# Inverses of the 32-row blocks made on VectorE, column by column, between the links of a running substitution

## What is computed

```python
s = jnp.einsum('bihd,bjhd->bhij', k, k) * scale
s = jnp.where(strict, s, -jnp.inf)          # strict: i > j
...
p = e / jnp.where(denom == 0, 1.0, denom)   # softmax over the strict lower triangle
L = p * beta.transpose(0, 2, 1)[..., None]
A = L + jnp.eye(T, dtype=L.dtype)[None, None]
u = jax.scipy.linalg.solve_triangular(A, v.transpose(0, 2, 1, 3), lower=True)
...
o = jnp.einsum('bhij,bjhd->bihd', attn, u).reshape(B, T, HID)
```

## Time and profile before

| | us |
|---|---|
| median of 3 runs | 886.89 |
| lowest and highest | 881.65, 887.53 |
| the profiled execution | 889.51 |
| its span | 887.7 |
| mean granted TensorE clock in it, share of full speed | 0.731 |

### The profile page before, as it was taken

The page is one execution under the profiler, slowest core; times in us unless marked ns, Lnnn a source line. Parts: engine busy times, 40 slices in busy tenths (PEclk is TensorE's granted clock), DMA queues, the critical chain, the costliest instruction groups (busy, mean ns, idle before and its releaser), DMA issues. The chain is left out here.

```text
span 887.7 us, 17573 instructions
## 1 busy us (share of the span) xinstructions
PE 531.0 (60%) x7316; PEld 409.8 (46%) x7316; DVE 570.7 (64%) x1036; ACT 279.6 (31%) x682; POOL 230.8 (26%) x322
## 2 busy tenths in 40 slices
PE   0343752445646499633655745765988672599981
PEld 0232532334434144432544434544665451599981
DVE  6679589659795958577671776256565238378743
ACT  3330242123144344005344052242412232245520
POOL 2000000000000000030582880860681007123444
PEclk9765875775665599865658757776868855699985
DMA  8442050041000100075005004120000052646314
GB/s 317 137 93 51 1 107 0 2 85 23 1 0 13 37 1 0 16 147 126 4 27 120 7 7 98 20 44 7 9 8 11 9 236 71 251 158 220 119 53 126
DMA packets 52064, 61.27 MB, mean 69 GB/s; under 512 B 25408, under 2 KB 45392, under 8 KB 47504
## 3 DMA queue, kind: packets, MB, share of 16 engines
q1 hardware_dynamic: 50176, 55.15, 23.0%
q0 software_dynamic: 1808, 4.99, 1.9%
HBM read 45.24 MB, written 13.63 MB: 66 GB/s over the span
## 5 line engine op out<-in xcount | busy, mean ns | idle before, releaser
L778 PE MATMUL psum<-arena 32*32 32x16 f32 (+20 forms) x5480 | 368.6, 280 | 251.1 <-DVE arena L1417 67.8
L778 PEld LDWEIGHTS psum<-arena 98*32 98x32 bf16 (+7 forms) x5480 | 265.4, 128 | 354.1 <-issue 104.2
L1851 POOL TENSOR_TENSOR arena<-arena 128x31 f32<-128x31 f32 (+15 forms) x124 | 67.5, 544 | 9.7
L1849 POOL TENSOR_TENSOR arena<-arena 128x31 f32<-128x31 f32 (+15 forms) x124 | 64.2, 518 | 9.7
L1206 ACT ACTIVATE arena<-psum 128x512 f32<-128x512 f32 (+1 forms) x48 | 35.4, 737 | 62.8 <-PE psum L778 62.5
L1402 DVE RECIPROCAL arena<-arena 128x512 f32<-128x512 f32 x16 | 53.6, 3353 | 0.5
L1237 ACT ACTIVATE psum<-psum,arena 128x256 f32<-128x256 f32 (+7 forms) x128 | 45.7, 371 | 26.2 <-DVE arena L1478 26.2
L1488 DVE TENSOR_REDUCE arena<-psum 128x2 f32<-128x512 f32 (+1 forms) x48 | 41.4, 862 | 18.6 <-PE psum L778 18.3
L1149 ACT ACTIVATE arena<-arena 128x255 f32<-128x255 f32 x64 | 27.1, 495 | 72.7 <-DVE arena L1380 72.7
L1394 DVE TENSOR_TENSOR_SCAN arena<-arena 128x255 f32<-128x255 f32 x64 | 42.6, 728 | 3.6 <-ACT arena L1149 3.4
L1862 POOL TENSOR_TENSOR fc_second_parts<-arena,fc_first_parts 128x2048 fp32r<-128x2048 f32 x6 | 27.9, 4651 | 64.1 <-ACT fc_first_parts L1305 64.1
(11 more groups left out here) (176 smaller groups left out, 917.9 us busy)
## 6 DMA issues: line engine op xcount, KB each, us to landing
arena<-fc SPq DMA_DIRECT2D x16, 1024.0 KB, 5.7
arena<-parts SPq DMA_DIRECT2D x40, 256.0 KB, 4.5
parts<-arena SPq DMA_DIRECT2D x16, 384.0 KB, 3.2
arena<-parts SPq DMA_DIRECT2D x40, 128.0 KB, 5.4
dispatched<-arena SPq DMA_DIRECT2D x1, 2048.0 KB, 18.4
arena<-arena SPq DMA_DIRECT2D x128, 8.0 KB, 1.8
arena<-dispatched SPq DMA_DIRECT2D x8, 256.0 KB, 3.2
expert_rows<-arena SPq DMA_DIRECT2D x8, 256.0 KB, 2.2
```

What stands on the lines that cost most here:

```text
L778: return nc.tensor.matmul(out, lhsT, rhs, start=start, stop=stop)
L1849: link(G_.tensor_tensor(tmp, A3[:, k + 1:BLK, k:k + 1].to_broadcast([P, rows, w]), X3[:, k:k + 1, 0:w].to_broadcast([P, rows, w]), ALU.mult))
L1851: ins = G_.tensor_tensor(X3[:, k + 1:BLK, 0:w], X3[:, k + 1:BLK, 0:w], tmp, ALU.add)
```

## The change

GpSimd's part of step `blocks` is taken out. VectorE's `blocks` now also clears blkX, sets its diagonal, and multiplies blkA by cT. The 31 columns of each batch become steps `("column", b, k)`, done by VectorE: those of batch 0 in a row, right ahead of its `inverse`; those of batches 1, 2 and 3 spread by `spread` over the chain of the batch before. `lag()` is the same as before and holds a column back as it does any other step that is not in its list. The semaphore `inverses_ready` is gone.

```diff
+        if b == 0:
+            o += [("column", 0, k) for k in range(BLK - 1)]
...
-        o += sum(spread(solve, ahead[b]), [])
+        columns = one_each(("column", b + 1, k) for k in range(BLK - 1)) if b + 1 < B else []
+        o += sum(spread(spread(solve, ahead[b]), columns), [])
...
                 elif kind == "blocks":
 
                     b = step[1]
-                    if b:
-                        dve.wait_ge(inv_ready, b)
                     wait_done(dve, ("kdiag", b), "act")
-                    st(V.transpose(cT, ncc[b]))
-                    st(V.transpose(blkA.rearrange("p (i j) -> p i j", i=BLK), diag.rearrange("p (n i) -> p i n", i=BLK)))
-                    settle()
-                    V.nop().then_inc(blocks_ready, 1)
+                    st(V.memset(blkX, 0.0))
+                    link(V.transpose(cT, ncc[b]))
+                    V.transpose(blkA.rearrange("p (i j) -> p i j", i=BLK), diag.rearrange("p (n i) -> p i n", i=BLK)
+                                ).then_inc(blocks_ready, 1)
+                    dve.wait_ge(blocks_ready, b + 1)
+                    st(V.memset(blkX[:, 0:BLK * BLK:BLK + 1], 1.0))
+                    link(V.tensor_tensor(A3, A3, cT.unsqueeze(2).to_broadcast([P, BLK, BLK]), ALU.mult))
+                elif kind == "column":
+
+                    k = step[2]
+                    rows, w = BLK - 1 - k, k + 1
+                    tmp = blkT[:, 0:rows * w].rearrange("p (i j) -> p i j", i=rows)
+                    link(V.tensor_tensor(tmp, A3[:, k + 1:BLK, k:k + 1].to_broadcast([P, rows, w]),
+                                         X3[:, k:k + 1, 0:w].to_broadcast([P, rows, w]), ALU.mult))
+                    link(V.tensor_tensor(X3[:, k + 1:BLK, 0:w], X3[:, k + 1:BLK, 0:w], tmp, ALU.add))
                 elif kind == "inverse":
 
                     b = step[1]
-                    dve.wait_ge(inv_ready, b + 1)
...
-                    if b and s == 0:
-                        dve.wait_ge(u_moved, 16 * HQ * NS * b)
+                    if s == 0:
+                        dve.wait_ge(*((u_moved, 16 * HQ * NS * b) if b else (pad_ready, 1)))
...
-                elif kind == "blocks":
-
-                    b = step[1]
-                    pool.wait_ge(blocks_ready, b + 1)
-                    if b:
-                        pool.wait_ge(invT_ready, b)
```

More of the change, by code:

```diff
@@ L416, in program @@
         top[0] = max(top[0], e_end)
+        A3, X3 = (f.rearrange("p (i j) -> p i j", i=BLK) for f in (blkA, blkX))
         def oraw(layer, b):
@@ L583, in program @@
         blocks_ready = sem("blocks_ready")
-        inv_ready = sem("inverses_ready")
         invT_ready = sem("inverses_T_ready")
```

## The result

The changed kernel takes 932.8 us (median of 4 runs, 929.17 to 934.34); the kernel before took 886.07 beside it (881.65 to 887.53). The ratio is 1.053, with a 95% interval of 1.048 to 1.058: 46.7 us slower. The forecast was 57 us (944, range 921 to 970). Direction and range held; the loss was oversized by about 10 us. In time alone 932.8 lies halfway between the forecast and the first rival (922), so the time does not choose between them; the profiles have to.

The account below looks back on a forecast made before the run. VectorE was taken as already the busiest compute engine beside TensorE. 23.3 + 2.4 + (13.2 - 4.1) + (11.3 - 2.5) + (13.8 - 1.9) - 1.0 + 2.5 = 57.0 us takes the median from 886.9 to 944 us, range 921 to 970.

Parts of the forecast that it names:

- first rival: In the chains, VectorE never idles while it has columns, delays using up later waits; +35, 922 us; chance 0.18.
- the 1.0 of credit: Before 485 us, ahead of `vproj`: VectorE instructions run faster without GpSimd beside them, about 1.0 us back.
- columns ahead of chain 1's `minus`: Two columns delay the `minus` that releases TensorE's transpose L905: +1.1 us.
- columns ahead of chain 2's `minus`: Four columns ahead of this `minus` add about 2.0 us.
- Batch 0: Its 31 columns between `vproj` and `inverse` are queued behind a 17.75 us wait and have no cover: +23.3 us.
- Price of a column: Two dependent VectorE instructions, 2 x 193 ns + 2 x 1.043 n ns: 0.45 to 0.92 us, 23.3 us a batch.
- second rival: Column elements cost 1.75 ns each in this layout, +7.7 us a batch: +29, 973 us; chance 0.16.
- Step `blocks`: VectorE's added clears and product take 2.4 us, uncovered only for batch 1, ahead of its first-link copies: +2.4 us.
- The walk over the waits: Columns checked wait by wait over 13 stretches per chain: 13.2, 10.2 and 11.8 us uncovered in chains 0, 1, 2.
- What is given back: VectorE's instructions speed up without GpSimd beside them: credits 4.1, 2.5, 1.9 us in chains 0 to 2, about 1.0 earlier.
- Clock: TensorE's busy share falls in the longer chains, so its granted clock may drop: guessed 0 to 8 us, taken +2.5.
- What was to be seen: Profile signs: VectorE busy 85 us more, first `inverse` 22 us later, TensorE idle over 25, chains about 62, 62, 44 us.

Follow-up runs that it names:

- no_columns: Changed kernel with all 124 columns left out on VectorE, clears and product with cT kept, so no engine inverts: 877.44 us, ratio 0.9934 to the kernel before.
- only0: Changed kernel with only batch 0 inverted on VectorE, batches 1 to 3 on GpSimd as before: 906.95 us, ratio 1.0248 to the kernel before.
- late: Changed kernel with batches 1 to 3 inverted on VectorE, batch 0 on GpSimd: 913.55 us, ratio 1.0335 to the kernel before.
- early0: Changed kernel with batch 0's columns moved forward, 6 behind batch 1's key maxima, 25 in front of batch 2's `vproj`: 908.65 us, ratio 1.0314 to before.
- placed: Changed kernel with columns of batches 1 to 3 hand-placed ahead of updates, the rest ahead of the inverse: 922.9 us, ratio 1.0472 to the kernel before.
- gpsimd_idle: Kernel before with GpSimd's inversion left out, GpSimd only clearing blkX: 870.93 us, ratio 0.985 to the kernel before.
- gpsimd_last: Changed kernel, batch 0's columns forward, others hand-placed, batch 3 on GpSimd, batch 1's `blocks` behind chain 0's first copies: 893.03 us, ratio 1.0123 to before.
- all_placed: Changed kernel, batch 0's columns forward, others hand-placed, a few shifted in chain 2, batch 1's `blocks` behind chain 0's first copies: 898.38 us, ratio 1.0217.

## Why the prediction was right, and where its sizes were off

Counted from the profiles behind `vproj`, the changed kernel lost 45.9 us (930.6 - 481.91 less 887.7 - 484.92). The prediction had 58.0 for the same, its sum without the 1.0 of credit ahead of `vproj`. (That credit was too small: from the small sum at 450.8 us to `vproj` it is 34.1 us before and 31.2 after, 3.0 back in this stretch alone.) So this account is 12 us apart, and the medians 10 on the first chip; where the changed kernel ran again it lost 52.9 us, 4 less than forecast. Part of the miss is thus what chips and executions differ by. `no_columns` lies between the two kernels and splits this: 55.2 for the columns, 9.3 given back net of `blocks`.

| term | predicted | measured |
|---|---|---|
| batch 0 | +23.3 | +23.4 |
| columns in chain 0 | +13.2 | +12.7 |
| columns in chain 1 | +10.2 | +7.9 |
| columns ahead of chain 1's `minus` | +1.1 | +1.8 |
| columns in chain 2 | +11.8 | +11.8 |
| columns ahead of chain 2's `minus` | +2.0 | +0.4 |
| clock, and the rest of the columns' time | +2.5 | -2.8 |
| `blocks` | +2.4 | +2.3 |
| credit, chains 0 to 2 | -8.5 | -10.9 |
| the rest of before against `no_columns` | 0 | -0.7 |

The columns' rows are the changed kernel less `no_columns` (for a chain 61.63 - 48.90, for a `minus` the time from the last copies to the next chain's first). The row on the clock holds -0.4 between chains 0 and 1 and -2.4 behind the first copies of the last chain. The latter is no more than executions differ by: the stretch from there to the end, in which all 13 profiles do the same work, takes 209.9 to 216.6 us.

How far single profiles carry this split is shown by the runs that repeat a part. With the columns spread, the chains repeat well: 61.1 to 61.6, 59.5 to 59.8 and 41.8 us in four profiles. The chains of before do not: by those of `only0` the net growth of chains 0 to 2 is 9.7, 7.4 and 10.2 us, where the earlier trace rows give 9.0, 5.0 and 7.5 and the sum had 9.1, 7.7 and 9.9; and the credit is 5.2 in place of 10.9. The net terms of chains 1 and 2 therefore fit, or are 2.7 and 2.4 too high, by which profile of the same work is the base, and the split of each into columns and credit is no surer. By medians what is given back net of `blocks` is 5.5 us (882.89 less 877.44), not 9.3.

- **Batch 0** was right, in size and in cause: `only0`, `late` and `early0` each show it.
- **Price of a column** was right: 425 ns at 256 elements, where the two rates gave 424, and means of 338 and 343 for 340. The second rival, dear elements, is out. The Trainium skill's "Advanced Engine Details and Errata", section "SBUF Cachelines", has a penalty for accesses that change their 16-byte line, which the additions' row starts would pay. Additions are 5 ns dearer than products on the mean, 0.6 us over all 124. The shape of 31 elements holds two cases: as 31 rows of one element an addition took 0.21 us, as one row of 31 it took 0.19. That is 0.02 us for 30 more row starts, which fits the 0.7 us a batch at the low end of the estimate.
- **Step `blocks`** was right in its sum. The clear took 0.91 us, between the two rates that I had (0.6 and 1.1), nearer to the one chosen.
- **The walk over the waits** was right for chain 0. In chain 1 it was too high by 2.3 against `no_columns`. A reason may be that a wait that was walked through once was not walked again with what the delays before it had done to TensorE, which is the slack of the first rival; no run shows it, and 2.3 us is also what chain 1 differs by between before and `only0`. In chain 2 the two 11.8 agree in part by luck: the walk started from waits at a clock of 0.78, and `no_columns` had 1.00 there, the changed kernel 0.81. VectorE's waits in chain 1 have not gone: 8.5 us are left ahead of copies, 5.4 of it before the first and so ahead of the chain's stretch, and 7.1 ahead of updates. The first rival (chains 0 and 1 all but free) is refuted for these two: they grew by 9.0 and 5.0 us net where it had 1.3 and nothing, and `placed` takes 9.4 and 5.0 us out of them by order alone, of which 1.3 and 2.5 come back behind them. For chain 2 it gave 7.9 less the 2.0 of the `minus`, 5.9; the net growth was 7.5. There VectorE is indeed all but saturated, and by the earlier trace rows the rival's arithmetic came nearer than the forecast's 9.9; by `only0`'s chain 2 (10.2) the forecast's did.
- **What is given back** was too small by 2.4 in the chains by the profile of before, and that is chain 2: it gave 4.3 where the sum had 1.9. By instruction the term was right: L1649 at 5.33 to 5.35 us for 28 in every chain, L1482 at 172 ns against 319. The difference in chain 2 goes with its granted clock, 1.00 in `no_columns`, which I had kept at the 0.78 of the earlier trace rows. With `only0`, whose chain 2 ran at 0.95, as the base it gave 1.7, near the 1.9.
- **Clock**: this term is the largest miss of the table, 5.3 of the 12 us, and it isn't borne out. Granted were 0.65, 0.72 and 0.81 after, for 0.69, 0.75 and 0.78 before; TensorE's busy time in the chains rose in chain 0 by 2.0 us and fell in chain 2 by 0.7. A loss of 2.5 us can't be read out of this, but it isn't excluded either: no run changed the clock by itself, so its own share stays open.
- **What was to be seen**: first inverse 23.8 us behind `vproj` (22 later was said; it is 23.4 later); TensorE idle 26.5 before its first solve (over 25 was said); chains 61.6, 59.5 and 41.8 (about 62, 62 and 44 was said); VectorE busy 76 us more (85 was said, with 9.5 us taken off for the interference, of which `gpsimd_idle` shows 13.1 in VectorE's busy time, 570.7 less 557.6).

## What to carry to other kernels

On an engine that works in order the place of added work sets its price: the same 31 columns cost 23 us behind a wait and ahead of the instruction that releases the next engine, and, moved ahead of that wait, some 21 us less. Spreading filler evenly over a chain isn't the same as placing it: find in the timeline which instruction waits and put the filler right in front of it, up to the length of the wait; where the filler exceeds the sum of the waits, as in chain 2, leave it on the engine that is idle. An idle engine that interferes a little (here 12 us over the kernel) is cheap beside adding 85 us of column instructions to the busiest one.

## What the runs showed of the hardware that was not expected

- The granted clock of chain 2 differed widely, and what sets it these runs don't show: 0.78 before, 1.00 in `gpsimd_idle`, 0.95 in `only0` and 0.89 in `gpsimd_last` (both with GpSimd at work beside it), 0.64 in `placed`. With nearly the same matmuls (581 to 598 records) TensorE's busy time was 29.7, 24.6, 25.5, 26.4 and 33.8 us. 1.00 is the 2.4 GHz level, and the other figures are stretches that mix it with 1.2 GHz. With the columns spread the chain's length did not follow it: 41.8 us each time, at 0.76 to 0.81.
- Executions part ways long before the change has any effect. Between 200 and 300 us the granted clock was 0.62 in the profiles of before, after and `gpsimd_last` and 0.74 in those of `no_columns` and `all_placed`. The rows of before and of `no_columns` (same columns as above):

```profile
200.00:300.00 100.00, 57.51 (x381) 40.14 (x381) 80.85 (x111) 32.19 (x55) 3.75 (x5) 0.62 0.06 15
```

```profile
200.00:300.00 100.00, 47.68 (x382) 35.66 (x381) 85.38 (x117) 37.19 (x68) 3.74 (x5) 0.74 0.05 12
```

The same number of matmuls takes 57.5 us in the one and 47.7 in the other, and `vproj` of batch 2 is reached at 475.8 us in `no_columns` and at 484.9 before, with nearly the same work ahead of it; at 478.8 in `all_placed` and at 486.3 in `gpsimd_last`, with the same order up to there. A comparison of single profiles on their spans would have been off by that much. Counted from `vproj` on, this part is out; what differs behind it (up to 2.6 us in a chain, up to 6.7 behind the last chain's first copies) is not.
